# Every engine's steps of a four-layer attention kernel put in another order, and its PSUM banks named in a table

## The reference

```python
# L0 and, with its own weights, L3: cross attention to ctx, with a residual
Q = query @ Wq + bq;  K = ctx @ Wk + bk;  V = ctx @ Wv + bv
query + softmax(Q @ K.T / 16) @ V @ Wo + bo

# L1: two attentions (a to ctx, v to side), layernorm on queries and on keys
out_a = cma(text, ctx, a_*);  out_v = cma(text, side, v_*)
output = out_a + out_v + text
_ln(output, ln_g, ln_b) @ fc_W + fc_b + output

# L2: keys and values from ctx; the softmax runs over the 128 queries
w = softmax(q @ k.T / 16, axis=queries);  x = w @ v + emb
_ln(x) * gamma + beta
```

## Time and profile before

| | |
|---|---|
| three runs | 576.27, 573.87, 575.56 us; median 575.56 |
| the profiled execution | 574.38 us, its span 572.1 us, mean granted TensorE clock 0.992 |
| TensorE busy | 554.0 us, 97% of the span, 4496 instructions |
| VectorE, ScalarE, GpSimd busy | 490.6 (86%), 442.7 (77%), 476.5 (83%) us |
| DMA | 77.62 MB, mean 136 GB/s |
| until the first group's Q_L1 | 43.49 us |

### The profile page before, as it was taken

The page is one execution under the profiler, slowest core; times in us unless marked ns, Lnnn a source line. Parts: engine busy times, 40 slices in busy tenths (PEclk is TensorE's granted clock), DMA queues, the critical chain, the costliest instruction groups (busy, mean ns, idle before and its releaser), DMA issues.

```text
span 572.1 us, 16196 instructions
## 1 busy us (share of the span) xinstructions
PE 554.0 (97%) x4496; PEld 537.5 (94%) x4496; DVE 490.6 (86%) x1506; ACT 442.7 (77%) x1534; POOL 476.5 (83%) x640
## 2 busy tenths in 40 slices
PE   8989999999999999999999999999999999999975
PEld 7889999999999999999999999999999999999964
DVE  0866999898999979988998989999999986998964
ACT  2769977888878796888869697967878886887553
POOL 3989978989979969988996999798988988394692
PEclk8989999999999999999999999999999999999999
DMA  7994457543676453584267363564644433323322
GB/s 239 369 277 125 117 124 173 154 117 102 158 162 155 122 129 84 153 210 128 67 158 193 118 148 107 141 166 101 187 109 107 95 91 95 93 57 84 87 53 74
DMA packets 174183, 77.62 MB, mean 136 GB/s; under 512 B 138896, under 2 KB 157712, under 8 KB 174096
## 3 DMA queue, kind: packets, MB, share of 16 engines
q1 hardware_dynamic: 174096, 76.59, 50.5%
HBM read 51.40 MB, written 25.17 MB: 134 GB/s over the span
## 4 chain that ended last, share of the span: by engine, by line
PE 91%; DVE 3%; ACT 2%; issue 2%; DMA 1%; SPq 0%; POOL 0%; DVEq 0%; ACTq 0%; POOLq 0%
PE bank L727 16%; PE bank L734 10%; PE bank L740 9%; PE bank L710 7%; PE bank L751 5%; PE bank L753 5%; PE bank L752 5%; PE bank L718 5%; PE bank L871 5%; PE bank L849 4%; PE bank L764 4%; PE bank L836 3%; PE bank L837 3%; PE bank L838 3%; ACT prob_L L987 1%
## 5 line engine op out<-in xcount | busy, mean ns | idle before, releaser
L987 ACT ACTIVATE prob_L<-bank,neg_max_L 128x128 f32<-128x128 f32 x320 | 115.0, 378 | 28.4 <-DVE neg_max_L L1296 27.7
L987 ACT ACTIVATION_READ_ACCUMULATOR prob_L<-bank,neg_max_L 128x1 f32 x320 | 69.2, 216 | 0.0
L1296 DVE TENSOR_REDUCE neg_max_L<-bank 128x2 f32<-128x256 f32 (+1 forms) x128 | 60.7, 479 | 9.5 <-PE bank L734 8.5
L1467 POOL TENSOR_TENSOR rstd_ln<-var_eps_ln,minus_half 128x2 f32<-128x2 f32 x64 | 45.2, 708 | 14.7 <-ACT var_eps_ln L997 14.4
L916 ACT ACTIVATE oT_hi_L<-bank 128x256 fp32r<-128x256 f32 (+1 forms) x96 | 45.1, 471 | 13.8 <-PE bank L740 13.1
L1133 DVE TENSOR_TENSOR oT_lo_L<-bank,oT_hi_L 128x256 fp32r<-128x256 f32 (+1 forms) x96 | 47.6, 501 | 8.2 <-ACT oT_hi_L L916 7.9
L916 ACT ACTIVATE probT_L<-bank 128x256 f32<-128x256 f32 (+1 forms) x96 | 44.1, 467 | 6.7 <-PE bank L718 6.5
L1520 POOL TENSOR_TENSOR x_bias<-x,bias_L 128x512 f32<-128x512 f32 x32 | 41.2, 1287 | 9.7 <-DVE x L1323 9.7
L1504 POOL TENSOR_TENSOR xT_lo_L<-x_in,xT_hi_L 128x512 fp32r<-128x512 f32 x32 | 41.2, 1286 | 8.6 <-ACT xT_hi_L L916 8.4
L1247 DVE BATCH_NORM_STATS2 stats_ln<-x 128x6 f32<-128x256 f32 x128 | 47.5, 414 | 0.2
L1513 POOL TENSOR_TENSOR x_bias<-x_in,bias_L 128x512 f32<-128x512 f32 x32 | 41.0, 1284 | 7.8 <-DVE x L1323 7.2
...
## 6 DMA issues: line engine op xcount, KB each, us to landing
...
keysT<-keys_out SPq DMA_DIRECT2D x128, 64.0 KB, 2.7
...
x3T<-x_out SPq DMA_DIRECT2D x128, 64.0 KB, 2.7
...
```

The source lines that it names most:

```text
L987: last = activation(at(prob[k], g)[:, b, :], block(bank, b), ACT.Exp, bias=at(neg_max[k], g)[:, b:b + 1], accum_out=at(total[k], g)[:, b:b ...
L1296: dve.tensor_reduce(at(neg_max[k], g)[:], scores, AX.X, ALU.max, negate=True).then_inc(done[f"max_{k}"], 1)
L1467: pool.tensor_tensor(at(rstd[k], g)[:], at(var_eps[k], g)[:], minus_half[:, 0:n], ALU.pow).then_inc(done[f"rstd_{k}"], 1)
```

## The change

STARTS and PREPARATIONS get other numbers in almost every row. The steps, what they do, their tiles and COPIES stay. `seats` no longer picks a bank; it takes the number from a new table SEATS, one for each use. The assertion behind it still demands that the bank's last user has been emptied earlier in the list, and the wait in `bank_for` is made as before. All lines below the tables move down by 49 (L727 becomes L776).

```diff
--- before.py
+++ after.py
...
-    "Q_L0": [1479, 3005, 3499, 4300, 4760, 7542, 8249, 9398, 10719, 11386, 12414, 14955, 16384, 17538, 19070, 22482, 23735,
...
+    "Q_L0": [1315, 2902, 3343, 4078, 4558, 7352, 8034, 9335, 10475, 11230, 12025, 14742, 16306, 17179, 18379, 22508, 23340,
...
-PREPARATIONS = {"run_up": 300, "k_L2": 1100, "M_L2": 925, "M_L1v": 2205, "N_L1a": 1822, "mean_M_L1v": 2435, "m_L1v": 2479, "M_L0": 1276,
...
+PREPARATIONS = {"run_up": 154, "m_L0": 1183, "M_L2": 687, "k_L2": 862, "n_L0": 1227, "M_L0": 1094, "N_L0": 1386, "n_fc": 1720, "N_L1a":
...
+SEATS = {
+    "m_L0": [3],
+    "M_L2": [0],
+    "k_L2": [1],
+    "n_L0": [4],
+    "M_L0": [2],
+    "N_L0": [6],
+    "Q_L0": [5, 1, 0, 0, 0, 5, 4, 1, 3, 4, 6, 6, 6, 4, 3, 1, 6, 5, 2, 2, 6, 5, 0, 3, 3, 1, 5, 3, 7, 7, 6, 6],
+    "S_L0": [7, 1, 7, 3, 4, 4, 4, 7, 5, 7, 4, 6, 1, 5, 2, 2, 7, 1, 6, 0, 4, 1, 7, 6, 7, 3, 1, 3, 4, 6, 0, 0],
...
+    "OUT_L3": [5, 3, 4, 2, 5, 3, 6, 1, 3, 5, 1, 6, 3, 0, 3, 3, 3, 4, 2, 3, 0, 2, 2, 6, 0, 4, 5, 5, 6, 3, 4, 3],
+}
...
     held, seat = [None] * BANKS, {}
     for _, g, name in table:
         if name in EMPTIED_BY:
-            n = min(range(BANKS), key=lambda b: -1 if held[b] is None else at[held[b]])
+            n = SEATS[name][max(g, 0)]
             assert held[n] is None or at[held[n]] <= at[name, g], f"no bank for {name} {g}"
             seat[name, g] = n, held[n]
             held[n] = EMPTIED_BY[name], g
```

More of the change, by code:

```diff
@@ L131 @@
-    "OUT_fc": [6264, 7100, 7927, 9257, 11108, 14133, 15101, 15928, 17184, 18721, 22160, 22692, 23806, 25300, 27642, 28927,
-        30976, 32504, 34406, 36117, 37021, 37934, 39558, 40969, 43555, 45760, 47066, 48269, 50020, 50824, 51601, 52303],
-    "out_fc": [6426, 7321, 8090, 9476, 11319, 14345, 15263, 16176, 17431, 18982, 22513, 22909, 23968, 25550, 28234, 29300,
[37 rows of a table removed]
-    "x_res": [9016, 9872, 11510, 12890, 14588, 17098, 18947, 19616, 21456, 21719, 25684, 26646, 27657, 28662, 31193, 32707,
[17 rows of a table removed]
-    "store": [10506, 11162, 12790, 14356, 16169, 18717, 20804, 21248, 23347, 24743, 27996, 28543, 29085, 30085, 33038, 34499,
[3 rows of a table removed]
@@ new lines @@
+    "hi_ctx": [1346, 1442, 1996, 3081, 3804, 4809, 5926, 7417, 7855, 9569, 11021, 12341, 16165, 17447, 19204, 20614, 22506,
[5 rows of a table added]
+    "lo_ctx": [1657, 1995, 3324, 4252, 5192, 5978, 7377, 8020, 9602, 11966, 13542, 16190, 17548, 19251, 20299, 22492, 24532,
+        25790, 27984, 30202, 31466, 31984, 33121, 33626, 36752, 37847, 39934, 40986, 42226, 44788, 45124, 46391],
+    "load_side": [406, 1414, 1846, 1990, 3218, 3551, 5418, 6343, 7192, 8512, 10418, 13206, 14126, 15100, 16255, 18277, 20903,
[5 rows of a table added]
+    "x_bias": [1431, 2224, 2621, 3932, 4941, 5066, 5529, 7157, 10341, 11088, 12224, 13416, 15461, 17227, 17884, 19782, 22297,
+        22940, 23946, 25862, 26639, 29330, 31271, 32323, 33333, 34620, 37290, 39542, 41780, 42492, 43879, 45491],
@@ new lines @@
+    "lo_fc": [5989, 6705, 7726, 8874, 10944, 13862, 14770, 15546, 16869, 18436, 21686, 22238, 23411, 24994, 27282, 28264, 30508,
+        31820, 33878, 35649, 36427, 37136, 38970, 40729, 43270, 45207, 46750, 47870, 49474, 50324, 51174, 51882],
+    "OUT_fc": [6074, 6910, 7805, 9005, 11045, 13965, 14884, 15640, 16948, 18591, 21917, 22579, 23526, 25103, 27381, 28409,
+        30624, 32116, 34086, 35753, 36556, 37228, 39362, 40888, 43407, 45420, 46860, 47974, 49701, 50505, 51282, 52005],
+    "out_fc": [6236, 7131, 7967, 9480, 11240, 14127, 15082, 15907, 17247, 18844, 22331, 22799, 23688, 25343, 27957, 28916,
[37 rows of a table added]
@@ new lines @@
+    "x_res": [8842, 9674, 11214, 12650, 14416, 16964, 18882, 19324, 21064, 21532, 25401, 26376, 27527, 28456, 30840, 32719,
[17 rows of a table added]
+    "store": [10562, 10930, 12476, 14078, 16207, 19109, 20550, 21112, 23263, 24154, 27745, 29066, 29162, 30105, 32968, 34484,
[3 rows of a table added]
+    "eps_keys": [1519, 2365, 2860, 3112, 4358, 5083, 5998, 7002, 7784, 9926, 11636, 13637, 14720, 15938, 17156, 18870, 21380,
[3 rows of a table added]
+    "eps_lnf": [5956, 6680, 7717, 8859, 10680, 13807, 14600, 15723, 16795, 18337, 21954, 22324, 23396, 24763, 27129, 28239,
[7 rows of a table added]
@@ new lines @@
+PREPARATIONS = {"run_up": 154, "m_L0": 1183, "M_L2": 687, "k_L2": 862, "n_L0": 1227, "M_L0": 1094, "N_L0": 1386, "n_fc": 1720, "N_L1a":
[14 rows of a table added]
+SEATS = {
[7 more added lines that the diff above has]
+    "S_L0": [7, 1, 7, 3, 4, 4, 4, 7, 5, 7, 4, 6, 1, 5, 2, 2, 7, 1, 6, 0, 4, 1, 7, 6, 7, 3, 1, 3, 4, 6, 0, 0],
+    "n_fc": [1],
[4 rows of a table added]
+    "mean_fc": [5],
[20 rows of a table added]
+    "T_fc": [2, 4, 2, 7, 7, 0, 0, 2, 4, 2, 6, 2, 1, 7, 3, 6, 4, 0, 5, 2, 4, 2, 2, 5, 3, 0, 0, 7, 4, 2, 6, 2],
+    "OUT_fc": [4, 2, 2, 7, 3, 0, 2, 7, 5, 1, 1, 6, 1, 7, 3, 5, 7, 6, 6, 6, 4, 3, 0, 5, 5, 0, 5, 7, 6, 6, 3, 0],
[8 rows of a table added]
+}
```

46 lines of the change are left out of this document (18 added, 28 removed), and 375 rows, old and new, of tables (PREPARATIONS, SEATS, STARTS).

## The result

The changed kernel takes 567.11 us (median of 6 runs, 566.32 to 568.76); the old one took 574.32 beside it (6 runs). The ratio is 0.9875, with a 95% interval of 0.9852 to 0.9897: 7.2 us less. The forecast was 570.5, its range 567.5 to 575.0. The profiled execution took 568.76 us (span 566.5), the slowest of the six, against 574.38.

What follows compares the result with a forecast made beforehand. TensorE, busy 97% of the span, was taken as the bound, so only its lost time counted. Gains of 2.9 + 0 + 1.6 = 4.5 us gave 569.9 (profiled) or 571.1 (median); 570.5 was taken, range 567.5 to 575.0.

Steps and rivals of the forecast that it cites:

- Middle: From 43.5 to 530 us: TensorE's 2.65 us idle stays the same, gain 0; bounds 2.0 won, 2.5 lost.
- standing wait: A layer's six matmuls wait for VectorE's xT_lo, 0.3 us in each of 29 groups: 579 us; chance 0.09.
- Start, part one: Loads and steps up to B2 of group 0: B2 at 19.3 against 18.69 us, a loss of 0.6.
- Start, part two: From B2 to the first Q_L1: two idles covered and the clock's fall gone, 3.5 us won.
- the clock falls once more: Fresh idles in the start lower TensorE's clock again, costing another 1.7 us: 572.2 us; chance 0.23.
- End: Last four groups: VectorE's earlier statistics remove GpSimd's idle before its rstd, 1.6 us won; bounds 0 and 2.8.
- Bank waits: New PSUM bank pattern: cost taken as 0, average reuse distance 8.0 steps in both orders; 1.2 us left in the range.
- Sum: Whole kernel, start, steady stretch and last groups together: 2.9 + 0 + 1.6 = 4.5 us won.

Runs made afterwards that it cites:

- changed_again: The changed kernel run again unaltered, on the same chip as the last four follow-up kernels: 566.76 us, ratio 0.9859 to the old kernel.
- three_moves: The old kernel with three VectorE steps placed one to three places earlier, every bank the same: 573.27 us, ratio 0.9973.
- the cut kernels: Old kernel with the new order only up to the first Q_L1, only behind it, or only behind group 29's OUT_fc; old bank rule: 574.89, 569.72, 573.17 us.
- filled_idles: The changed kernel with 7 more matmuls on a constant in TensorE's idle time between 6.7 and 10.8 us: 566.46 us, ratio 0.9844.

## Why the prediction was wrong in size

**"Middle. I take the same sum, 0."** This is the step that failed: 3.3 us were won there in the profile beside the result, 4.5 in that of changed_again. It alone puts the result outside the range (567.1 + 3.3 is 570.4). I had read the profile's 2.65 us of idle time as all that could be won, and set the bound at 2.0. The stalls were 7.3 us. Of these 3.1 stood behind VectorE, mostly its low parts, which is the place of my "standing wait", with the other sign, and 2.1 behind exponentials that still held a bank. three_moves shows that stalls of the first kind are worth their size, the cut kernels that the order of the steady stretch removes them whatever the start. The forecast of 570.5 also starts from 575.0 for the old kernel, whose median over six runs is 574.3: that is 0.7 of the 3.4 us between forecast and result.

**Start, part one.** The chain was right and the clock was not in it. I said M_L0 11.5, S_L0 15.7, N_L1a 17.5, B2 19.3. With the clock kept up they came at 11.15, 15.21, 17.40 and 19.01; in the changed kernel at 10.79, 17.42, 18.91 and 20.53. I had not seen that the columns' load, gone behind x, would hold up k_L2. So 1.84 us were lost up to B2 (20.53 against 18.69), not 0.6.

**Start, part two.** The 30 steps took 21.39 us (41.92 - 20.53) against 24.80: 3.4 won, as forecast (3.5). But 1.71 of it was the clock, and that was counted wrongly: the same low stretch stood at 12 to 18 us instead. In other profiles of the old start these steps take 23.6 us (43.45 - 19.87; 43.11 - 19.56). The order's own part is 2.2, 23.6 less 21.4. Net at the first Q_L1 it is 1.57, not 2.9.

**The rival "the clock falls once more"** is what the trace shows for the start, and it did not decide, since the old kernel paid the same 3.4 us elsewhere. The Trainium skill's rule ("TensorE: Matmul & The Clock Gate", section "What's actually happening"), that activity releases a throttle that is otherwise on, agrees with filled_idles: the same program with work in its idle time stayed at 1.00 through the start. That every new idle time brings a low stretch does not come out of the runs: filled_idles kept 1.00 over waits of 1.40 and 1.51 us.

**End.** 1.30 won, 1.6 forecast; GpSimd's idle time before the rstd is gone as told, and 0.3 was over-counted.

**Bank waits.** I took 0 for the table and looked only at how far apart a bank's uses stand. That number is the same under both orders and says nothing: at such distances the old rule made 2.1 us of waits under the old order, and under the new one three of 0.41 to 0.74. The table is worth 0.9 to 1.6 us, a part of the gain that I had not seen at all.

**Sum.** In the two profiles: 1.57 + 3.32 + 1.30 = 6.2 us at the last OUT_L3, less 0.6 behind it. That 0.6 is the clock again. It fell to 0.50 at 561.4 us, during this very product, whose six matmuls took 1.53 us instead of 0.97:

```profile
561.50:562.00 0.50, 0.50 (x4) 0.50 0.00 0
```

With the 1.4 us stall behind the late send it is enough to make this profiled execution the slowest of six. In changed_again, whose profiled execution is the median one, neither is there: 1.76 + 4.53 + 1.31 = 7.6 us at the last OUT_L3, and 7.6 in the span (564.5 against 572.1). The medians fell by 7.2 and 8.1.
